# Local attention layers on one core: the key tile's sums of squares go ahead of the query tile's cosine product on VectorE

## The reference, cut to what matters

```
q, k, v = split(shift_tokens(x) @ Wqkv)            # 16 heads of 64
q = l2norm(q) * q_scale;  k = l2norm(k) * k_scale
q = q * cos * scale + rotate_half(q) * sin * scale
k = k * cos / scale + rotate_half(k) * sin / scale
# windows of 32 tokens; each looks at itself and at the window before
sim  = einsum(bq, bk2) * 8, masked
out  = einsum(softmax(sim), bv2)
x = out @ Wo + x
x = ffn(shift_tokens(x)) + x
```

## Time and profile before

| | us |
|---|---|
| median of 3 runs | 3284.66 (3282.99 to 3294.11) |
| the profiled execution | 3291.8 |
| its span | 3290.0 |
| busy in it: TensorE | 2842.4 (86%) |
| VectorE | 2679.5 (81%) |
| ScalarE | 2142.6 (65%) |
| GpSimd | 1372.2 (42%) |

### The profile page before, as it was taken

One profiled execution on the slowest core, in us unless ns is written; L12 is line 12 of the kernel. 1 busy time (PEld: TensorE's weight loads), 2 busy tenths in 40 slices (PEclk: granted clock), 3 DMA queues, 4 the chain that ended last, 5 costly groups with the idle time before them and its releaser, 6 DMA issues. The chain is left out here.

```text
span 3290.0 us, 73875 instructions
## 1 busy us (share of the span) xinstructions
PE 2842.4 (86%) x29085; PEld 1576.1 (48%) x29181; DVE 2679.5 (81%) x4028; ACT 2142.6 (65%) x3276; POOL 1372.2 (42%) x811
## 2 busy tenths in 40 slices
PE   3999888888888889859988998899899889988998
PEld 1233233332333333326754665566466646755664
DVE  4999888888478789459977997899699879978995
ACT  2377677676745656637766775677477657766774
POOL 0200432425224200056644663666366636645661
PEclk8699999999978989879999999999999999999999
DMA  3200001010000010011111111111011101111110
GB/s 108 66 2 2 1 7 30 8 30 1 23 16 2 16 22 2 20 57 40 34 48 33 34 34 41 40 34 47 28 40 40 54 21 40 34 48 33 34 40 20
DMA packets 62986, 101.11 MB, mean 31 GB/s; under 512 B 20450, under 2 KB 45216, under 8 KB 61472
## 3 DMA queue, kind: packets, MB, share of 16 engines
q1 hardware_dynamic: 62636, 96.26, 10.5%
HBM read 38.30 MB, written 7.34 MB: 14 GB/s over the span
## 5 line engine op out<-in xcount | busy, mean ns | idle before, releaser
L841 DVE TENSOR_REDUCE a_part<-ps 128x1 f32<-128x512 f32 (+3 forms) x1664 | 989.0, 653 | 213.0 <-PE ps L546 204.7
L821 ACT ACTIVATE a_Pb<-ps 128x1024 f32<-128x1024 f32 (+3 forms) x832 | 762.3, 973 | 378.4 <-PE ps L707 376.5
L1225 PE MATMUL ps<-l_w_qkv,l_XS 128*128 128x512 f32 x1152 | 562.5, 623 | 118.4 <-DVE l_qn L1600 81.3
L546 PE MATMUL ps<-a_KS,a_QS 48*128 48x512 bf16 (+3 forms) x1664 | 475.4, 400 | 85.1 <-DMA a_QS<-pieces 37.0
L1163 POOL TENSOR_TENSOR l_sine<-l_qn,l_tab 128x512 f32<-128x512 f32 x192 | 343.6, 1790 | 248.9 <-DVE l_qn L1600 241.1
L1187 POOL TENSOR_TENSOR l_weights<-l_weights,l_rcp 128x1024 f32<-128x1024 f32 x96 | 182.6, 1903 | 487.9 <-DVE l_rcp L1637 487.9
L1225 PEld LDWEIGHTS ps<-l_w_qkv,l_XS 128*128 128x128 f32 x1152 | 206.2, 193 | 348.0 <-issue 151.8
L1587 DVE TENSOR_REDUCE l_bounded<-l_square 128x8 f32<-128x512 f32 x384 | 252.3, 678 | 106.9 <-ACT l_square L1436 89.7
L707 PE MATMUL ps<-a_QS,a_KS 50*128 50x512 bf16 (+3 forms) x1664 | 284.6, 385 | 61.4 <-ACT a_gate_up L755 15.7
L546 PEld LDWEIGHTS ps<-a_KS,a_QS 48*128 48x128 bf16 x1664 | 123.2, 96 | 429.5 <-DVE a_part L841 340.3
L1436 ACT ACTIVATE l_square<-ps 128x512 f32<-128x512 f32 x384 | 228.5, 598 | 134.6 <-PE ps L1225 133.9
(11 more groups left out here) (217 smaller groups left out, 4583.2 us busy)
## 6 DMA issues: line engine op xcount, KB each, us to landing
l_V_earlier<-l_V SPq DMA_DIRECT2D x96, 384.0 KB, 3.5
l_V_earlier<-l_V SPq DMA_DIRECT2D x96, 128.0 KB, 3.4
l_w_qkv<-in_L_ffn_Wqkv_dram SPq DMA_DIRECT2D x6, 1536.0 KB, 8.3
a_QS<-pieces SPq DMA_DIRECT2D x96, 64.0 KB
a_KS<-pieces SPq DMA_DIRECT2D x60, 64.0 KB
pieces<-a_piece SPq DMA_DIRECT2D x6, 512.0 KB, 2.6
pieces<-a_work SPq DMA_DIRECT2D x12, 256.0 KB, 2.7
l_w_o<-in_L_ffn_Wo_dram SPq DMA_DIRECT2D x6, 512.0 KB, 4.6
```

What stands on the lines that cost most here:

```text
L546: mm = e.matmul(bank[:, 0:width], QS[rows, c, pair, qt * P:(qt + 1) * P], KS[A][rows, pair, b * CH:b * CH + width], start=not masked, stop ...
L821: e.activation(Pb[:, n % 2, 2 * p:2 * p + 2, lo:CH], ps[:, 2 * p:2 * p + 2, lo:CH], ACT.Exp)\
L841: e.tensor_reduce(part[:, u % 2, column(h, qt), b:b + 1], bank[:, 0:width], AX.X, ALU.max)\
L1225: e.matmul(ps[:, (V_BANK[T] if i == 2 else 0) + b, :], XS[:, T * P:(T + 1) * P], w_qkv[:, at:at + CH], start=True, stop=True).then_inc(s.v ...
```

## The change

In a round, VectorE used to make the cosine product of the queries (tile `T + 2`) right after it had normalised them. Now it leaves that to the next round, where the same tile is `T + 1`, and makes it after `residual` and after the sums of squares of that tile's keys. The call for a layer's tile 1 stays where it was, in the round of tile 0, and so do the calls for tile 0. Nothing else moves on any engine.

```diff
                         if ahead:
                             sum_squares(l, T + 1, 1)
+                        if T and ahead:
+                            cosines(l, T + 1, 0)
                         if T:
                             place_high(l, T - 1, 0)
                         if ahead:
                             normalise(l, T + 1, 1)
                         maxima(l, T)
                         subtract(l, T)
                         if T + 2 < NT:
                             sum_squares(l, T + 2, 0)
                         if ahead:
                             cosines(l, T + 1, 1)
                             add_rotated(l, T + 1)
                         sums(l, T)
                         if T + 2 < NT:
                             normalise(l, T + 2, 0)
-                            cosines(l, T + 2, 0)
```

## The result

| | before | after |
|---|---|---|
| median, us | 3287.31 (4 runs, the three above and one more; 3282.99 to 3294.11) | 3323.5 (4 runs, 3315.73 to 3331.2) |
| ratio to before | | 1.0113, 95% interval 1.0091 to 1.0135 |
| the profiled execution, us | 3291.8 | 3315.73 |
| round of tiles 0 to 13, us | 15.44 | 16.00 and 15.85 in turn |

The changed kernel is 1.1% slower, 36 us between the medians; 3311 was forecast, with 3287 to 3340 as its range.

What follows compares the result with a forecast made beforehand. A ring through VectorE, TensorE and ScalarE was taken to bound the round; late `place_high` delays `values` by 0.25 + 0.05 + 0.03 = 0.33 us, 78 times: 26 us on 3284.66, 3311 us, range 3287 to 3340.

Steps and rivals of the forecast that it cites:

- The ring: Queries normalised, TensorE from key to query projection, ScalarE's squares, VectorE's second part: this closed chain sets the 15.44 us round.
- The product ready 4.18 us after the queries' normalising began: Moved cosine product on VectorE: ready at 2119.87, held by GpSimd's second sine piece, ending 1.08 us after it at 2121.30.
- `place_high` starts about 0.08 us before the end of the instruction in front of it, as `residual` did.: VectorE's copy behind the moved product: starts at 2121.22, ends at 2121.92, 0.75 us later than before.
- The second wait, "I allow 0.03": TensorE's queue ahead of `values`: a second wait behind the first, not priced by the rows, allowed 0.03 us.
- The sum: Whole kernel: 78 rounds x 0.33 us = 26 us, giving 3311 us against the median, 0.8% slower.
- the first group: First group of four of `values` on TensorE: takes 0.34 us and not 0.29, another 0.05 us.
- The waits with room: Other waits in the round: `subtract` about 0.65 us later, still ahead of the squares; value projection's loss covered by TensorE's idle time.
- the rival in which all of VectorE's delay reaches the ring: Much slower: the round's-end idle time is used up, 0.6 to 0.75 us a round, 3332 to 3343 us; chance 12%.
- the 0.81 us at the round's end: TensorE's idle time until VectorE has normalised the queries; if gone in the later profile, the forecast is too low.
- Tile 14 at nothing: Round of tile 14: value projection some 0.65 us later, covered by TensorE's 1.82 us wait for GpSimd's weights; cost nothing.
- The groups of the whole span: Sign over the whole profile: busy time of the cosine products, L1608, falls from 290.6 us to about 254.
- The faster rival: VectorE and GpSimd set the round, which shrinks by up to 0.44 us: 34 us in all, 3250 us; chance 7%.

Runs made afterwards that it cites:

- e1_high_first: The changed kernel with `place_high` put ahead of the moved cosine product: 3294.89 us, 1.0021 of the kernel before.
- e5_high_after_keys: The kernel before with only `place_high` moved, to behind the keys' normalising: 3421.9 us, 1.0408 of the kernel before.
- e4_keys_cosine_early: The kernel before with the keys' cosine product put ahead of the next queries' sums of squares, into VectorE's idle time: 3228.52 us, 0.9805 of before.
- e3_short_sine: The changed kernel with GpSimd's second sine piece for the queries of tiles 2 to 15 cut from 32 columns a head to 2: 3305.43 us, 1.0039 of before.
- e2_halves_swapped: The changed kernel with VectorE copying partitions 0 to 63 of the first half of `wT` and ScalarE 64 to 127: 3319.87 us, 1.0097 of before.

## Why the prediction came out slightly low

- *The ring.* Right. e1_high_first and e5_high_after_keys show that the late `place_high` carries the loss in the rounds, e4_keys_cosine_early that the ring is the bound.
- *The product ready 4.18 us after the queries' normalising began, ended 1.08 us behind the second sine piece.* Right to the hundredth: 2121.21 - 2117.03 = 4.18, and 1.08. By the delay of the Trainium skill ("SBUF — State Buffer", section "A bandwidth-pool intuition that's wrong (but worth ruling out)") it would have ended at about 2121.57 + 0.115 + 1.22 = 2122.91, an estimate; measured 2122.65, so going by the rows was right. The case in which the Trainium skill measured that delay is another one, a transfer that GpSimd describes behind a VectorE copy. Without a hold it ran 1.22 us (e3_short_sine).
- *"`place_high` starts about 0.08 us before the end of the instruction in front of it, as `residual` did."* This step failed. The pattern was `residual` behind a product, both starting at partition 0. The copy starts at partition 64 and comes 0.03 after: 0.11 us more. The kernel before shows it already. The instruction in front of its copy of the earlier trace rows ends at 2120.43, and the copy starts at 2120.47:

```profile
2120.25 0.18 DVE L1589 TENSOR_REDUCE l_norm<-l_bounded 128x16 f32<-128x32 f32 x1
```

  The Trainium skill states the rule ("VectorE: DVE Perf Modes", section "Two Vector instructions with no wait between them"): an instruction that reads or writes SBUF or PSUM from another group of 32 partitions on than the last one to do so there starts only when all earlier ones have finished. e2_halves_swapped agrees with it, 0.13 us in a round; the prediction did not apply it.
- *The second wait, "I allow 0.03".* Mis-sized: 0 in one tile, 0.15 in the next. In the tiles of even number in the loop layers (40 of 96) TensorE's queue has two wait instructions in front of `values`, L1283 for VectorE's copy and L1285 for ScalarE's, which was done long before; in all other tiles one, L1285, takes VectorE's copy. Counts, shortest, median and longest ns in after:

```profile
L1283 PEldq EVENT_SEMAPHORE  x40: 51/51/51, 1461.4 to 2940.6; - x40
```

```profile
L1285 PEldq EVENT_SEMAPHORE  x56: 202/866/1417, 1476.5 to 3257.2; - x56
L1285 PEldq FUSED_REGOPS  x40: 51/51/65, 1461.5 to 2940.7; - x40
```

  In tiles 0 to 13 the copy's end and `values` lie 0.26 us apart with two (0.27 in the first of a layer) and 0.10 with one, in after and in e5_high_after_keys alike, and 0.10 for even and odd tiles of the sixth layer. The row that priced this wait at 0.11 is that of an odd tile.
- *The sum.* 0.25 as reckoned + 0.11 for the held copy + 0.05 for the first group = 0.41 us, + 0.15 in every second tile = 0.56. The rounds rose by 0.41 and 0.56, those of the sixth layer by 0.42. The mean of a loop layer is 0.485 instead of 0.33, which makes the 37 us instead of 26. Another 2.6 us between 3311 and 3323.5 are the median of before, which rose with its fourth run.
- *The waits with room.* `subtract` ended 10.06 us after the queries' normalising began instead of 9.25, 0.81 later (0.65 was reckoned; the rest is the held copy and the held instruction behind it), still ahead of the squares, with 0.44 and 0.29 us to spare in turn. So the rival in which all of VectorE's delay reaches the ring did not come about: the 0.81 us at the round's end are still there.
- *Tile 14 at nothing.* Right in the five loop layers: its round took 14.47 to 14.50 us, 14.45 to 14.47 before. In the sixth it took 14.48 for 14.17, 0.3 us that stay unexplained. Of the idle times of the earlier trace rows the first grew and the second shrank:

```profile
2302.35 1.98 PE L1225 MATMUL ps<-l_w_qkv,l_XS 128*128 128x512 f32 x4 [1.58 <-DVE l_weights L1628]
...
2308.91 1.09 PE L1274 MATMUL ps<-ident,l_weights 128*128 128x128 f32 x8 [1.05 <-POOL l_weights L1187]
```

- *The groups of the whole span.* L1608 fell to 257.4 us, where about 254 was forecast:

```profile
L1587 DVE TENSOR_REDUCE l_bounded<-l_square 128x8 f32<-128x512 f32 x384 | 261.1, 685 | 184.5 <-ACT l_square L1436 164.2
...
L1163 POOL TENSOR_TENSOR l_sine<-l_qn,l_tab 128x512 f32<-128x512 f32 x192 | 260.8, 1359 | 249.4 <-DVE l_qn L1600 241.7
...
L1608 DVE TENSOR_TENSOR l_cosine<-l_qn,l_tab 128x1024 f32<-128x1024 f32 x192 | 257.4, 1341 | 6.7 <-POOL l_tab L1178 5.5
```

The faster rival is the one that these rows might have tempted one to: GpSimd's sine pieces lost 83 us and the cosine products 33, and the kernel became slower. That time lay beside the ring; the idle time in front of L1587 took it up (106.9 us before, 184.5 after).

## What to carry to other kernels

With two engines over 90% busy, follow the waits around one round until they close, and ask of a moved instruction only whether it makes something on that ring later. Put a movable instruction into an idle time that lies *on* the ring (here the queries' squares: 2% faster) rather than taking it out of a place where it covered a wait beside it. And when a start time is copied from a pattern row, look at whether its partitions and waits are the same.

## What the runs showed of the hardware that was not expected

- A VectorE copy at partitions 64 to 127, between instructions that start at partition 0, began 0.03 us after its predecessor's end instead of 0.08 before it, and the one behind it too: 0.11 us at each end, with or without a sine piece of GpSimd beside it. With the halves swapped both overlaps of 0.08 are back.
- A second wait instruction in TensorE's queue, for a semaphore that was up long before, went with 0.15 us more from the awaited copy's end to the matmul (0.26 against 0.10), where TensorE stood idle for that copy. No run takes the instruction out by itself; the sixth layer, which lacks it, has 0.10 throughout.
